# Self attention of a fused decoder: sums kept by unit and divided at the end, next scores given out behind the weighted sum, maximum and exponential each in two parts

## The reference, cut to what matters

```
def _mha(x, ctx, mask, qw, qb, kw, kb, vw, vb):      # here x = ctx, mask = None
    q = _split_heads(x @ qw + qb)                    # 16 heads of 8 features
    k = _split_heads(ctx @ kw + kb)
    v = _split_heads(ctx @ vw + vb)
    scores = jnp.einsum('bqhd,bkhd->bhqk', q, k) / np.sqrt(D // H)
    probs = jax.nn.softmax(scores, axis=-1)
    out = jnp.einsum('bhqk,bkhd->bqhd', probs, v)
    return out.reshape(x.shape[0], x.shape[1], D)
...
sa = _mha(x, x, None, sq_w, sq_b, sk_w, sk_b, sv_w, sv_b)
x = _self_output(sa, x, so_w, so_b, so_g, so_be)     # projection, residual, layer norm
inter = jax.nn.gelu(x @ fi_w + fi_b, approximate=False)
```

## Time and profile before

| | |
|---|---|
| median of 3 runs | 3595.74 us (3588.3 to 3598.84) |
| the profiled execution, its own time | 3594.51 us |
| span of the profiled execution, first to last instruction | 3592.7 us |
| mean granted TensorE clock | 0.826 |
| busy over the span: PE, PEld, DVE, ACT, POOL | 70%, 47%, 48%, 29%, 10% |
| busy from 2053 to 2135 us, a self attention stage: PE, DVE, ACT | 57.46, 46.72, 34.10 of 82 us |

### The profile page before, as it was taken

How to read it: one execution, slowest core, us unless ns; L and a number is a source line. 1 busy time by engine, 2 the same in 40 slices (tenths; PEclk the granted TensorE clock), 3 DMA queues, 4 the chain that set the end, 5 groups by cost and what they waited for, 6 DMA issues and landing times.

```text
span 3592.7 us, 51054 instructions
## 1 busy us (share of the span) xinstructions
PE 2516.7 (70%) x20359; PEld 1695.8 (47%) x20374; DVE 1733.0 (48%) x4213; ACT 1030.5 (29%) x1406; POOL 346.3 (10%) x596
## 2 busy tenths in 40 slices
PE   4555258778877887357566779677796777967778
PEld 3343046666665665334444444444444444444444
DVE  5545735546545553541337542475514754157541
ACT  3333412222222221011122343223432233222432
POOL 0101000000000000036200100110001100011000
PEclk8777558878877887578787899888998899988999
DMA  2000000000000000202530000000000000000000
GB/s 76 0 0 0 2 1 1 7 7 7 2 7 7 7 1 7 87 19 27 120 88 1 1 7 1 1 1 1 7 0 1 1 1 7 0 1 1 1 1 24
DMA packets 39195, 47.95 MB, mean 13 GB/s; under 512 B 7153, under 2 KB 36353, under 8 KB 38210
## 3 DMA queue, kind: packets, MB, share of 16 engines
q1 hardware_dynamic: 33346, 40.43, 3.8%
q0 software_dynamic: 5632, 4.33, 0.9%
HBM read 31.81 MB, written 12.91 MB: 12 GB/s over the span
## 4 chain that ended last, share of the span: by engine, by line
issue 49%; PE 28%; DVE 14%; POOL 4%; ACT 2%; DMA 1%; SPq 0%; POOLq 0%; DVEq 0%; ACTq 0%
PE banks L2302 6%; PE banks L859 5%; DVE weights L2024 2%; PE banks L2291 1%; PE banks L559 1%; PE banks L908 1%; PE banks L2227 1%; DVE xs L888 1%; PE banks L570 1%; PE banks L1923 1%; DVE dilvals L880 1%; POOL rstd L897 1%; DMA conv<-wide_area 1%; PE banks L1144 1%; POOL dilvals L897 1%
## 5 line engine op out<-in xcount | busy, mean ns | idle before, releaser
L880 DVE BATCH_NORM_STATS2 stats<-banks 128x6 f32<-128x128 f32 x208 | 46.3, 284 | 349.4 <-PE banks L859 290.3
L2195 DVE TENSOR_REDUCE wide_area<-banks 128x8 f32<-128x2048 f32 x64 | 146.6, 2291 | 107.3 <-PE banks L2115 107.3
L2167 ACT ACTIVATE weights<-banks 128x2048 f32<-128x2048 f32 x64 | 120.1, 1877 | 121.5 <-PE banks L2128 121.5
L895 POOL TENSOR_TENSOR rstd<-moments,eps 128x4 f32<-128x4 f32 x56 | 11.1, 199 | 1414.5 <-DVE moments L884 1414.5
L908 PE MATMUL banks<-wA,xs 128*128 128x128 f32 x208 | 55.8, 372 | 114.4 <-DVE xs L888 114.0
L1688 DVE TENSOR_REDUCE wide_area<-banks 128x16 f32<-128x1024 f32 x80 | 94.1, 1218 | 59.7 <-PE banks L1601 59.7
L880 DVE BATCH_NORM_STATS2 dilvals<-banks 128x6 f32<-128x128 f32 x144 | 32.0, 285 | 185.7 <-PE banks L859 183.2
L1144 PE MATMUL banks<-wC,weights 128*128 128x72 f32 x512 | 89.9, 358 | 18.0 <-ACT weights L1184 18.0
L1144 PEld LDWEIGHTS banks<-wC,weights 128*128 128x128 f32 x512 | 87.7, 270 | 24.5 <-ACT weights L1184 24.5
L908 PE MATMUL banks<-wA,gates 128*128 128x128 f32 x144 | 37.0, 347 | 84.3 <-DVE gates L888 83.4
L908 PEld LDWEIGHTS banks<-wA,xs 128*128 128x128 f32 x208 | 26.7, 172 | 138.4 <-DVE xs L888 136.0
(11 more groups left out here) (746 smaller groups left out, 6412.7 us busy)
## 6 DMA issues: line engine op xcount, KB each, us to landing
big<-in_wE SPq DMA_DIRECT2D x1, 4096.0 KB, 13.2
weights<-long_kernel SPq DMA_DIRECT2D x8, 512.0 KB, 8.8
conv<-wide_area SPq DMA_DIRECT2D x16, 256.0 KB, 6.9
wC<-in_wC SPq DMA_DIRECT2D x1, 3012.0 KB, 16.9
wC<-in_wG SPq DMA_DIRECT2D x1, 2971.0 KB, 19.4
big<-in_wT SPq DMA_DIRECT2D x1, 2816.0 KB, 9.9
x_all<-in_xT SPq DMA_DIRECT2D x1, 2048.0 KB, 10.4
rows<-spread SPq DMA_DIRECT2D x8, 256.0 KB, 3.1
```

Of the source, the lines that this page charges most:

```text
L880: dve.bn_stats(m.stats[:, i, :], self.tokens(i)).then_inc(*sg.up("dve", f"stats{i}"))
L2167: act.activation(m.weights, bank[:, :, :].rearrange("p r c -> p (r c)"), ACT.Exp, scale=DK ** -0.5)\
L2195: dve.tensor_reduce(m.peaks[:, k % 2, :, :].rearrange("p t (r c) -> p r t c", r=4)[:, :, :, SPARE[j]], bank[:, :, :].rearrange("p r (t k) ...
```

## The change

The `norm` of each unit goes out of the loop. ACT now copies the weighted sum of unit k to a place of its own (`sums[k]`: three work areas and `xs`, halves of 256 columns), and after the eighth unit 16 transposes (four for each token tile, `back0` to `back3`, into banks 0 to 3), four reciprocals of 16 elements and four products of 128 elements a partition do the division. `z_tokens` is four transposes that wait for one `norm` each.

The next unit's scores no longer wait for `norm`. They are given out right behind `out` of the same lane, in two parts: `first_scores` (r = 1, 2, 3), one tick, and `scores` (r = 0) one tick later, which waits for the copy of bank 0. The maximum is two instructions (1536 and 512 elements a partition). `turned` is given out in the order r = 0, 1 and then r = 2, 3 with a semaphore for each; the exponential is two instructions of 1024 elements; `out` is r = 0, 1 behind the first exponential and r = 2, 3 behind the second. The number of ticks stays 42. On PE a unit's ticks are row, turned, out, `first_scores`, `scores` of the next; PE's stream in the middle reads row x, `first_scores` y, turned x, `scores` y, out x, then with x and y exchanged. On ACT the two exponentials and the copy take ticks 3, 4 and 5 of a unit (before: exponential 3, copy 4), and `af` comes one tick later than before (42 in place of 41).

```diff
-    TICKS = 1 + 5 * len(ORDER) + 1
+    TICKS = 2 + 5 * len(ORDER)
...
+        def ahead(first, then):
+            return " ".join([each(1, *first)] + [" ".join(f"{name}{k + d}" for name, d in then) for k in range(units)]).split()
+
+        later = {f"{name}{units}" for name in ("scores", "first_scores", "max", "first_max")}
+        pe = ahead(("first_scores", "scores"), [(name, 0) for name in ("row", "first_turned", "turned", "out")] + [("first_scores", 1), ("scores", 1)])
+        dve = ahead(("first_max", "max"), [("query", 0), ("first_max", 1), ("max", 1)])
+        self.sig = Section(clock, pe="k q v " + " ".join(x for x in pe if x not in later) + " " + tile_steps("back", "z_tokens") + " z",
+                           act="k q v " + each(units, "first_exp", "exp", "copied") + " af", pool="blank",
+                           dve="keys0 keys2 keys1 keys3 " + " ".join(x for x in dve if x not in later) + " " + each(NT, "recip", "norm"))
+
+    def scores(self, pe, n, k, bands):
+        m, (b, j) = self.lane, self.ORDER[k]
+        for i in range(2):
+            for r in bands:
+                rows = slice(32 * r, 32 * r + 32)
+                mm = pe.matmul(m.bank[:, r, i * S:(i + 1) * S], m.qf[rows, (2 * b + i) * P:(2 * b + i + 1) * P],
+                               m.selfkeys[rows, j, b * S:(b + 1) * S], start=True, stop=True)
+        return mm
+
+    def turned(self, pe, k, bands):
+        m, (b, j) = self.lane, self.ORDER[k]
+        for i in range(2):
+            for r in bands:
+                rows = slice(32 * r, 32 * r + 32)
+                mm = pe.matmul(m.bank[:, r, i * S:(i + 1) * S], m.selfkeys[rows, j, (2 * b + i) * P:(2 * b + i + 1) * P],
+                               m.query[rows, 0, :], start=True, stop=True)
+        return mm
+
+    def out(self, pe, k, bands):
+        m, (b, j) = self.lane, self.ORDER[k]
+        for i in range(2):
+            for r in bands:
+                at = ((2 * b + i) * H + 4 * r + j) * (DK + 1)
+                mm = pe.matmul(m.bank[32 * r:32 * r + 32, 0, 0:S], m.selfflat[:, at:at + 32],
+                               m.weights[:, (2 * r + i) * S:(2 * r + i + 1) * S], start=(i == 0), stop=(i == 1))
+        return mm
...
+        pe.wait_ge(*sg.done("act", "v", n))
+        pe.wait_ge(*sg.done("dve", f"keys{self.ORDER[0][1]}", n))
+        self.scores(pe, n, 0, range(1, 4)).then_inc(*sg.up("pe", "first_scores0"))
+        self.scores(pe, n, 0, range(1)).then_inc(*sg.up("pe", "scores0"))
+        yield
         for k, (b, j) in enumerate(self.ORDER):
...
+            self.turned(pe, k, range(2)).then_inc(*sg.up("pe", f"first_turned{k}"))
+            self.turned(pe, k, range(2, 4)).then_inc(*sg.up("pe", f"turned{k}"))
+            yield
+            pe.wait_ge(*sg.done("act", f"first_exp{k}", n))
+            self.out(pe, k, range(2))
             pe.wait_ge(*sg.done("act", f"exp{k}", n))
-            for i in range(2):
-                for r in range(4):
...
+            self.out(pe, k, range(2, 4)).then_inc(*sg.up("pe", f"out{k}"))
+            yield
+            if k == last:
+                break
+            if b == 0:
+                pe.wait_ge(*sg.done("dve", f"keys{self.ORDER[k + 1][1]}", n))
+            self.scores(pe, n, k + 1, range(1, 4)).then_inc(*sg.up("pe", f"first_scores{k + 1}"))
...
+            self.scores(pe, n, k + 1, range(1)).then_inc(*sg.up("pe", f"scores{k + 1}"))
+        pe.wait_ge(*sg.done("act", f"copied{last}", n))
+        for t in range(NT):
+            for k, (b, j) in enumerate(self.ORDER):
+                if t // 2 == b:
+                    mm = pe.transpose(bank[:, t, j * P:(j + 1) * P], m.sums[k][:, t % 2 * P:(t % 2 + 1) * P], m.ident)
+            mm.then_inc(*sg.up("pe", f"back{t}"))
+        yield
+        for t in range(NT):
+            pe.wait_ge(*sg.done("dve", f"norm{t}", n))
+            pe.transpose(bank[:, 0, t * P:(t + 1) * P], m.heads[:, t, :], m.ident).then_inc(*sg.up("pe", f"z_tokens{t}"))
         yield
...
-        yield
+        yield from idle(2)
         for k in range(len(self.ORDER)):
+            yield
+            act.wait_ge(*sg.done("pe", f"first_turned{k}", n))
+            act.activation(m.weights[:, 0:2 * T], bank[:, 0:2, :].rearrange("p r c -> p (r c)"), ACT.Exp, scale=DK ** -0.5)\
+               .then_inc(*sg.up("act", f"first_exp{k}"))
+            yield
+            act.wait_ge(*sg.done("pe", f"turned{k}", n))
+            act.activation(m.weights[:, 2 * T:4 * T], bank[:, 2:4, :].rearrange("p r c -> p (r c)"), ACT.Exp, scale=DK ** -0.5)\
+               .then_inc(*sg.up("act", f"exp{k}"))
+            yield
+            act.wait_ge(*sg.done("pe", f"out{k}", n))
+            act.activation(m.sums[k], bank[:, 0, 0:S], ACT.Copy).then_inc(*sg.up("act", f"copied{k}"))
             yield from idle(2)
-            act.wait_ge(*sg.done("pe", f"turned{k}", n))
-            act.activation(m.weights, bank[:, :, :].rearrange("p r c -> p (r c)"), ACT.Exp, scale=DK ** -0.5)\
-               .then_inc(*sg.up("act", f"exp{k}"))
-            yield
-            act.wait_ge(*sg.done("pe", f"out{k}", n))
-            act.activation(m.outT[:, 0:S], bank[:, 0, 0:S], ACT.Copy).then_inc(*sg.up("act", f"copied{k}"))
-            yield from idle(2)
-        act.wait_ge(*sg.done("pe", "z_tokens", n))
+        act.wait_ge(*sg.done("pe", f"z_tokens{NT - 1}", n))
         act.activation(m.af[:, :], bank[:, 0, :], ACT.Identity, bias=self.cols["v"]).then_inc(*sg.up("act", "af"))
-        yield
...
+        dve.wait_ge(*sg.done("pe", "first_scores0", n))
+        self.peak(dve, 0, slice(1, 4)).then_inc(*sg.up("dve", "first_max0"))
+        dve.wait_ge(*sg.done("pe", "scores0", n))
+        self.peak(dve, 0, slice(0, 1)).then_inc(*sg.up("dve", "max0"))
+        yield
         for k, (b, j) in enumerate(self.ORDER):
...
+            if k == last:
+                break
+            dve.wait_ge(*sg.done("pe", f"first_scores{k + 1}", n))
+            self.peak(dve, k + 1, slice(1, 4)).then_inc(*sg.up("dve", f"first_max{k + 1}"))
+            yield
+            dve.wait_ge(*sg.done("pe", f"scores{k + 1}", n))
+            self.peak(dve, k + 1, slice(0, 1)).then_inc(*sg.up("dve", f"max{k + 1}"))
+            yield
+        for t in range(NT):
+            out, recip = bank[:, t, :].rearrange("p (j r e) -> p r j e", r=4, e=32), m.recips[:, t, :, :]
+            dve.wait_ge(*sg.done("pe", f"back{t}", n))
+            dve.reciprocal(recip, out[:, :, :, DK]).then_inc(*sg.up("dve", f"recip{t}"))
+            dve.wait_ge(*sg.done("dve", f"recip{t}", n))
+            dve.tensor_tensor(m.heads[:, t, :].rearrange("p (r j e) -> p r j e", r=4, e=DK), out[:, :, :, 0:DK],
+                              recip.unsqueeze(3).broadcast_to([P, 4, 4, DK]), ALU.mult).then_inc(*sg.up("dve", f"norm{t}"))
...
+            kept = [*lane.work[2:5], lane.xs.rearrange("p t d -> p (t d)")]
+            lane.sums = [area[:, i * S:(i + 1) * S] for area in kept for i in range(2)]
+            lane.recips = lane.smalls[:, 0:NT * H].rearrange("p (t r j) -> p t r j", t=NT, r=4)
```

More of the change, by code:

```diff
@@ L2095, in pe @@
+    def out(self, pe, k, bands):
[6 more added lines that the diff above has]
+        return mm
     def pe(self, pe, n, x_ready, biased_ready):
         m, sg, w = self.lane, self.sig, self.w
-        bank = m.bank
+        bank, last = m.bank, len(self.ORDER) - 1
@@ L2131, in pe @@
+            self.turned(pe, k, range(2, 4)).then_inc(*sg.up("pe", f"turned{k}"))
             yield
+            pe.wait_ge(*sg.done("act", f"first_exp{k}", n))
+            self.out(pe, k, range(2))
             pe.wait_ge(*sg.done("act", f"exp{k}", n))
-            for i in range(2):
-                for r in range(4):
-                    at = ((2 * b + i) * H + 4 * r + j) * (DK + 1)
-                    mm = pe.matmul(bank[32 * r:32 * r + 32, 0, 0:S], m.selfflat[:, at:at + 32],
-                                   m.weights[:, (2 * r + i) * S:(2 * r + i + 1) * S], start=(i == 0), stop=(i == 1))
@@ L2138, in pe @@
-            mm.then_inc(*sg.up("pe", f"out{k}"))
+            self.out(pe, k, range(2, 4)).then_inc(*sg.up("pe", f"out{k}"))
[5 more added lines that the diff above has]
+            self.scores(pe, n, k + 1, range(1, 4)).then_inc(*sg.up("pe", f"first_scores{k + 1}"))
             yield
             pe.wait_ge(*sg.done("act", f"copied{k}", n))
-            for i in range(2):
-                mm = pe.transpose(bank[:, 1, i * P:(i + 1) * P], m.outT[:, i * P:(i + 1) * P], m.ident)
@@ L2143, in pe @@
-            mm.then_inc(*sg.up("pe", f"back{k}"))
+            self.scores(pe, n, k + 1, range(1)).then_inc(*sg.up("pe", f"scores{k + 1}"))
             yield
-        pe.wait_ge(*sg.done("dve", f"norm{len(self.ORDER) - 1}", n))
-        for i in range(NT):
-            mm = pe.transpose(bank[:, 0, i * P:(i + 1) * P], m.heads[:, i, :], m.ident)
-        mm.then_inc(*sg.up("pe", "z_tokens"))
+        pe.wait_ge(*sg.done("act", f"copied{last}", n))
```

(7 more changed lines are left out.)

27 lines of the change are left out of this document (1 added, 26 removed).

## The result

The changed kernel takes 3609.43 us (median of 10 runs, 3603.06 to 3613.95), the kernel before 3595.68 (10 runs, 3586.95 to 3600.68). The ratio is 1.0042, 95% interval 1.0033 to 1.0052: slower by 0.3 to 0.5%. The forecast was 3613. The profiled execution has a span of 3606.8 us, 14.2 more than before, and a mean granted clock of 0.824 (0.826).

A forecast was written before the change was run, and what follows sets the result against it. No engine was taken as full; the order of short steps and the waits between them bound the kernel. (0.2 + 0.4 + 3.9) x 4 = +18 us gave a forecast of 3613 us, range 3585 to 3636 (own case 3602 to 3624).

The forecast's parts named there:

- the ring: Repeating chain of steps between the two lanes in a self attention stage: forecast +0.4 us a stage over 14 half rings.
- Half ring: Time from one lane's row to the other lane's next row: 5.47 us forecast against 5.44 before, +0.03.
- Row to first_scores 0.37 and the last wait: On PE, row x to first_scores y 0.37 us; second half of out to row y 1.00 us.
- The two exponentials: On ACT, 1.02 us each with some 0.05 overlap: the pair takes 2.0 us in place of 1.88.
- Turned's start: On PE, turned x starts only after first_scores y, at 1.34 us after row, though its query allows 1.01.
- the second rival: Between row and turned, and out and row, waits shrink: half ring 4.74 us, kernel faster at 3572; chance 0.15.
- Turned's halves abreast: On PE, turned's second half (r = 2, 3) runs abreast with its first, at no added time.
- The serial rival: Turned's halves run one behind the other on PE: half ring 5.8 us, +19 us in all, 3632; chance 0.17.
- Ramp: Start of a stage: split maximum of unit 0 and a later first lane-1 row cost +0.2 us a stage.
- End of the stage: After lane 1's last row: lane 0's scaling +2.3, lane 1's z behind the Gelu +1.6; 3.9 us a stage stay, uncovered.
- a sign of being wrong: Forecast is wrong if last row to lane 1's z grows under 2 us, or half rings come under 5.3.
- The third rival: Later sublayers absorb the end's delay in idle time; only some 1.5 us a stage stay: 3600; chance 0.23.

The follow-up runs named there:

- run 7: Kernel before with turned's eight matmuls given out by row group, both of r = 0 first, then both of r = 1 and so on: ratio 1.0001.
- run 10: Kernel before plus unread filler transposes in three PE gaps a lane behind the stage, 24 in lane 0's first gap, 12 in the others: ratio 0.9957.
- runs 9: Changed kernel plus 12 unread filler transposes in each of three PE gaps a lane behind the stage: ratio 0.9978, median 3582.28 us.
- filled ones: Kernels before and changed with unread filler transposes in PE's gaps behind the stage: ratios 0.9957 (24 in lane 0's first gap) and 0.9978 (12 everywhere).
- run 1: Kernel before with the bulk division alone: sums kept by unit, 16 transposes and four divisions at the end, scores, maximum and exponential undivided: ratio 1.0072.
- run 3: Changed kernel with turned, exponential and out each undivided again, the rest as changed: ratio 1.0110, 3634.94 us.

## Why the prediction was right, point by point

The number was right, and the largest term nearly so. That the sum came so near is in part luck: the ring had the wrong sign, and two effects that the forecast put at nothing, the clock (+10.0) and what is given back later (-6.6), partly cancelled.

- *Half ring, 5.47 forecast, 5.37 measured.* Row to first_scores 0.37 and the last wait 0.98 (0.37, 1.00) were right. The two exponentials follow at 0.92 and last 1.94 in all, where 2.0 was taken. Turned's start was wrong: it begins at 1.01 beside first_scores, as the second rival had it, but the exponential starts only 0.04 earlier than forecast, since turned's row groups 1 to 3 still have matmuls of first_scores before them (the row at 2078.07). So the ring gave 0.90 us a stage (76.13 against 75.23 for its 14 half rings) instead of costing 0.4. The second rival named the mechanism and priced it at up to 0.33 a half ring, where it gave 0.04.
- *Turned's halves abreast:* right. The serial rival (5.8) fell, here and in run 7, and with it the rule of strict program order of the Trainium skill ("TensorE: Matmul & The Clock Gate", Part 3). The row by which the prediction argued is of a weight load, which proves nothing of matmuls. The row that does is the one below, of the kernel before. Its four matmuls start within 0.03 us, all ahead of the first of L1601 at 1994.68, though three of L1601's stand ahead of the fourth in the program.

```profile
1994.56 0.31 PE L1599 MATMUL banks<-whole_h 3*128 3x256 bf16 x4
```

- *Ramp +0.2:* from the stage's start to lane 1's last row is 98.92 before and 98.12 after, so beside the ring's 0.90 it cost 0.1.
- *End of the stage +3.9:* z of lane 0 at 6.61 (6.66), the scaling at 11.86 (12.3), `af` of lane 1 behind the Gelu. As measured against the plain kernel before, z of lane 1 is only 2.3 later (1.47 in the second stage, under the 2 that the prediction named as a sign of being wrong), because that kernel ran its first feed forward group at lowered clock. Against the same kernel at full clock (run 10) it is 3.5.
- *Two readings of the rows* were wrong, without harm to the sum. `norm` starts 0.10 into the following turned and ends 0.32 into it (2063.75), not 0.1. And "issue" in the chain is time in which the engine waited for nothing that the profile shows, not time in which nothing runs.
- *"No cover that I can find, so the 3.9 us stay":* this failed. Shown: of 6.55 us at lane 1's up, 3.58 are order (runs 9 and 10) and 2.97 are clock: the low stretch costs the kernel before 3.64 there (61.00 against 57.36) and the changed one 6.61 (67.55 against 60.94). Then some 2 us are given back before the next stage. That happens in the next iteration's earlier sublayers: at its first matmul (L1532) the changed kernel is still 6.4 behind (134.45 and 140.87 after the last row).

The account over the span of the two profiled executions, +14.2: 1.6 less before the loop, which the change doesn't touch; 1.9 less from the stages' starts to their last rows (3.5, had the kernel before not been 1.6 shorter there in its second iteration alone); four times 4.7 to 6.6 up to lane 1's up, 24.3, of which 14.3 (4 x 3.58, the first stage's taken for all) are order and 10.0 clock; 6.6 given back behind it, three times 2.1 and 0.2 behind the last stage. The forecast was 15.6 for the order, 0 for the clock, 2.4 for ring and ramp, 0 given back.

The third rival, the absorbed end, was in part true: about a quarter of the delay is given back in the plain kernels, and most of it after three of the four stages in the traces of the filled ones. What it didn't see was that the clock adds before that.

## What to carry to other kernels

Before an edit takes work off TensorE in a latency-bound loop, look at the granted clock of the loop and of what follows: a pair of unread transposes a unit was worth 20 us in run 1's kernel, and filler in the gaps 1% of the kernel before. To price an order of work, bring both kernels to the same clock first; a difference of two plain traces mixes the two. And follow the difference to the end of the program: what is late at one place can be given back further on. When an instruction moves one tick, follow both lanes' copies of it.

## What the runs showed of the hardware

- The granted clock can fall inside a regular loop and come back: 5.44 becomes 7.0 us a half ring at 0.76, at the same places in every stage. Why it is the fifth and eleventh half ring in run 1, and the seventh to tenth in run 3, is not explained.
- The same 16 matmuls of out given out in two halves, with the exponential and turned in two, kept the clock at 1.00 in all 56 half rings; in one piece it fell in 16 of them. The use of that split was the clock, not the ring (5.37 against 5.36). Why the order of the same matmuls matters to the clock is not explained.
- The mean clock of a kernel is a poor guide: 0.824 after and 0.826 before, with 10 us between them from where the low stretches lie.
